# Finding queries without a key by a minimum in the mask instruction of VectorE, with a mask of 0 and 1, scaled queries and reordered instruction lists

## What is computed

```
x = x + attention(layernorm(x), ctx, ctx, mask)      # x 32x56x128, ctx 32x1500x128
x = x + ffn(layernorm(x), w1, w2)                     # 128 -> 512 -> 128, gelu, quantised

q = split(query @ Wq + bq); k = split(ctx @ Wk + bk); v = split(ctx @ Wv + bv)   # 16 heads of 8
scores = q @ k.T / sqrt(8)
scores = where(mask == 0, -1e9, scores)               # mask is int32, 32x1x56x1500
probs  = softmax(scores)
out    = (probs @ v) @ Wo + bo
```

## Time and profile before

| | us |
|---|---|
| median of three executions | 962.15 |
| lowest and highest | 957.84, 962.29 |
| the profiled execution, its own time | 959.75 |
| its span in the profile | 958.0 |

### The profile page before, as it was taken

The page is one execution under the profiler, slowest core; times in us unless marked ns, Lnnn a source line. Parts: engine busy times, 40 slices in busy tenths (PEclk is TensorE's granted clock), DMA queues, the critical chain, the costliest instruction groups (busy, mean ns, idle before and its releaser), DMA issues.

```text
span 958.0 us, 33628 instructions
## 1 busy us (share of the span) xinstructions
PE 887.8 (93%) x11716; PEld 694.2 (72%) x11716; DVE 753.1 (79%) x2593; ACT 673.4 (70%) x1272; POOL 231.5 (24%) x253
## 2 busy tenths in 40 slices
PE   3767989999999999999999999999999999999983
PEld 2344767777787787778787777777787777778772
DVE  3687568888788878888788888888787888888744
ACT  2543667777887877777886777777887777777661
POOL 6310142230222222130222222131222222031200
PEclk9788999999999999999999999999999999999997
DMA  5520221122222211122222211122222111220000
GB/s 130 127 62 1 63 61 29 42 57 60 63 60 63 59 34 47 46 60 60 63 60 63 53 32 50 51 60 60 63 60 61 49 32 50 56 60 0 4 2 6
DMA packets 59375, 49.34 MB, mean 52 GB/s; under 512 B 2785, under 2 KB 55633, under 8 KB 59345
## 3 DMA queue, kind: packets, MB, share of 16 engines
q1 hardware_dynamic: 57551, 48.11, 19.0%
q10 hardware_dynamic: 1793, 0.83, 0.4%
HBM read 47.91 MB, written 0.92 MB: 51 GB/s over the span
## 4 chain that ended last, share of the span: by engine, by line
issue 66%; POOL 18%; PE 7%; DVE 5%; ACT 1%; DMA 1%; POOLq 1%; DVEq 0%; ACTq 0%
POOL k_lo L573 8%; POOL qry_hi L565 4%; POOL qry_lo L566 4%; PE ps_p L820 2%; DMA ctx_sb<-in_ctx_dram 1%; PE ps_p L803 1%; DVE max_junk L1091 1%; POOL q_lo L563 1%; POOL q_hi L562 1%; PE ps_v L856 1%; PE ps_p L744 1%; ACT probs L659 1%; POOL x_rows L581 0%; PE ps_p L741 0%; POOLq L556 0%
## 5 line engine op out<-in xcount | busy, mean ns | idle before, releaser
L1091 DVE CUSTOM_DVE_ANT_0 max_junk<-ps_p,mask_bias 120x500 bf16<-120x500 f32 x768 | 481.6, 675 | 125.3 <-PE ps_p L803 104.5
L659 ACT ACTIVATE probs<-ps_p 125x448 f32<-125x448 f32 x768 | 359.3, 551 | 87.0 <-PE ps_p L820 81.6
L573 POOL TENSOR_TENSOR k_lo<-k_full,k_hi 128x500 fp32r<-128x500 f32 x96 | 119.8, 1262 | 592.0 <-ACT k_hi L651 587.2
L856 PE MATMUL ps_v<-probs,vals 125*32 125x112 f32 x6144 | 162.9, 262 | 0.8 <-issue 0.4
L803 PE MATMUL ps_p<-k_hi,qry_hi 64*120 64x500 f32 x768 | 148.8, 413 | 15.6 <-POOL qry_hi L565 6.5
L820 PE MATMUL ps_p<-qry_hi,k_hi 64*125 64x448 f32 x768 | 158.6, 403 | 4.4 <-DVE seg_max L1091 1.7
L856 PEld LDWEIGHTS ps_v<-probs,vals 125*32 125x32 f32 x6144 | 146.9, 111 | 21.1 <-issue 17.7
L641 ACT ACTIVATE k_full<-ps_p,bk_sb 128x500 f32<-128x500 f32 x96 | 64.7, 674 | 123.1 <-PE ps_p L744 122.6
L820 PE MATMUL ps_p<-own_query,mask_bias 57*125 57x448 f32 x768 | 145.7, 368 | 0.0
L820 PE MATMUL ps_p<-qry_lo,k_hi 64*125 64x448 f32 x768 | 144.4, 366 | 0.0
L820 PE MATMUL ps_p<-qry_hi,k_lo 64*125 64x448 f32 x768 | 144.3, 365 | 0.0
(11 more groups left out here) (124 smaller groups left out, 831.5 us busy)
## 6 DMA issues: line engine op xcount, KB each, us to landing
ctx_sb<-in_ctx_dram SPq DMA_DIRECT2D x31, 750.0 KB
mask_sb<-in_mask_Bx1xSxS_ik_dram SPq DMA_DIRECT2D x64, 328.1 KB
own_query<-shift SPq DMA_DIRECT2D x64, 1.8 KB
out_dram<-x_rows SPq DMA_DIRECT2D x16, 56.0 KB, 1.6
ctx_sb<-in_ctx_dram ACTq DMA_DIRECT2D x1, 750.0 KB
x_rows<-in_x_dram SPq DMA_DIRECT2D x1, 672.0 KB, 10.9
w_sb<-in_L_ffn_w_dram SPq DMA_DIRECT2D x2, 256.0 KB, 8.8
x_rows<-in_x_dram SPq DMA_DIRECT2D x1, 224.0 KB, 5.9
```

The costliest lines, as they stand in the source:

```text
L573: pool.tensor_tensor(k_lo[:, p, at], k_full[:, (p + n) % 2, :], k_hi[:, p, at].bitcast(F32), ALU.subtract)\
L659: act.activation(probs[:, c % NP, h], ps_p[0:KC, BANK[how]["S", c, h], 0:HC], ACT.Exp)\
L856: mm = pe.matmul(ps_v[r:r + VT, col:col + PAIR], vals[:, p, c, t].rearrange("p a r -> p (a r)"), src, start=(c == 0 and t < 4), stop=(c == ...
L1091: dve.tensor_tensor_reduce(max_junk[0:MROWS, BANK[how][slot], :], ps_p[0:MROWS, BANK[how][slot], 0:SEG], mask_bias[0:MROWS, p, s * SEG:(s ...
```

## The change

ScalarE no longer sums the mask. The instruction that turns the mask into a bias also keeps a minimum: it now writes 1 where the mask is 0 and 0 elsewhere, and the minimum over the segment is 1 only if every key is masked. A reduction over the three segments gives `some_key` (which is now 1 for a dead query), and the diagonal `some_diag` is made by one comparison, `ident > some_key`, which is 1 on the diagonal where the query is alive. So `some` now stands behind the third bias of its batch and no longer waits for ACT.

Since the mask is 1 and not -2^30, everything that is added to the scores is brought to that scale: the queries are multiplied by 2^-30 when they are made, the maxima are made with a subtraction, `own_query` has -1 on its diagonal in place of 1 (a second constant, `neg_ident`), `shift` is a plain copy, and ACT's exponential has the scale 2^30.

```
             def bias_mask(bt, n):
...
-                dve.tensor_scalar(mask_bias[0:MROWS + 1, p, at], mask_sb[0:MROWS + 1, p, at], 0.0, -BIG,
-                                  ALU.is_equal, ALU.mult).then_inc(mask_biased, 1)
+                dve.tensor_scalar(mask_bias[0:MROWS + 1, p, at], mask_sb[0:MROWS + 1, p, at], 0.0, None,
+                                  ALU.is_equal, ALU.min, accum_out=all_masked[0:MROWS + 1, n:n + 1])\
+                    .then_inc(mask_biased, 1)
             def find_some(bt):
...
-                dve.wait_ge(mask_summed, b + 1)
-                dve.tensor_scalar(some_key[0:SQ, :], mask_sum[0:SQ, :], 0.5, None, ALU.is_gt)\
-                    .then_inc(some_found, 1)
+                dve.wait_ge(mask_biased, NSEG * (b + 1))
+                dve.tensor_reduce(some_key[0:SQ, :], all_masked[0:SQ, :], AX.X, ALU.min).then_inc(some_found, 1)
                 dve.wait_ge(some_found, b + 1)
-                dve.tensor_scalar(some_diag[0:SQ, :], ident[0:SQ, 0:SQ], some_key[0:SQ, 0:1], None, ALU.mult)\
+                dve.tensor_scalar(some_diag[0:SQ, :], ident[0:SQ, 0:SQ], some_key[0:SQ, 0:1], None, ALU.is_gt)\
                     .then_inc(some_diag_ready, 1)
...
-            def sum_mask(bt):
-
-                b, k, p = bt
-                act.wait_ge(mask_loaded[p], 32 * (k + 1))
-                wait(act, some_found, b)
-                act.activation(mask_sum_junk[0:SQ, :], mask_sb[0:SQ, p, :], ACT.Abs,
-                               accum_out=mask_sum[0:SQ, :]).then_inc(mask_summed, 1)
...
-                act.activation(probs[:, c % NP, h], ps_p[0:KC, BANK[how]["S", c, h], 0:HC], ACT.Exp)\
+                act.activation(probs[:, c % NP, h], ps_p[0:KC, BANK[how]["S", c, h], 0:HC], ACT.Exp, scale=BIG)\
...
-                                      bq_sb[:, 0:1], float(HD) ** -0.5, ALU.add, ALU.mult).then_inc(q_copied, 1)
+                                      bq_sb[:, 0:1], float(HD) ** -0.5 / BIG, ALU.add, ALU.mult).then_inc(q_copied, 1)
...
-                                         ALU.add, ALU.max, seg_max[0:MROWS, 4 * h + r, s:s + 1])\
+                                         ALU.subtract, ALU.max, seg_max[0:MROWS, 4 * h + r, s:s + 1])\
...
+            put(pool.memset(neg_ident[:], 0.0))
+            put(pool.affine_select(out=neg_ident[:], in_=neg_ident[:], compare_op=ALU.not_equal, fill=-1.0,
+                                   base=0, pattern=[[-1, 128]], channel_multiplier=1))
```

```
 DVE_EVEN = order("""
-    own0 m0 m1 m2 m3 m4 m5 m6 m7 m8 m9 bias0 m10 m11 m12 m13 D0 m14 m15 m16 m17 m18 m19 O0 some0 bias1 m20 m21
-    m22 m23 F0 neg0 rows0 R0 rows1 bias2
+    own0 D0 m0 m1 m2 m3 m4 m5 m6 m7 bias0 m8 m9 m10 O0 m11 m12 m13 m14 m15 bias1 m16 m17 m18 m19 bias2 some0 m20
+    m21 m22 m23 neg0 rows0 R0 F0 rows1
...
 POOL_EVEN = order("""
-    kl0 q0 kl1 kl2
+    kl0 kl1 kl2 q0
```

## The result

The changed kernel takes 1011.87 us (median of four runs, 1010.64 to 1013.2), the kernel before 961.01 on the same chip: a ratio of 1.0535, 95% interval 1.0503 to 1.0566. It is 51 us slower. My forecast was 954.5, between 933 and 970.

What follows compares the result with a forecast made beforehand. TensorE, 93% busy, was nearest its limit; VectorE's chain ended the even half, PE's list the odd. 959.75 - 1.5 (loop) - 6.0 (filling) = 952.25 us, put at 954.5 against the median; range 933 to 970.

Steps and rivals of the forecast that it cites:

- the last one of the odd half: From R0 to the next M0 on PE: T1 and 0.25 idle go, D0 (0.3) and 0.45 for own0 enter, 3.1 us.
- rival of mine: Three: row chain slips through, 935 us, 0.34; mask instruction costs 0.9, 970 us, 0.14; no change, 961 us, 0.10.
- The mask instruction: VectorE's mask instruction with accumulated minimum: 0.60 us from start to start, before 0.33; 1.2 us a pass, by cost table 1.6.
- the shared port: VectorE and GpSimd share an exclusively locked port pair; a mask instruction losing its double rate would stop being held.
- The lock: Even half: POOL's last k_lo, qry_hi and qry_lo hold VectorE's row chain, so M0 comes at 27.0 us, before 27.4.
- the 1.0 I left: Even half: VectorE's idle time among its list, 1.0 us where before it was 2.1, putting neg at 18.3 us.
- The pass without the jump: One pass of the loop: 54.1 us, 0.1 less than before, so -1.5 us over 14 passes.
- The even half: From even M0 to odd M0, ended by VectorE's row chain under POOL: 27.0 us, before 27.4.
- The odd half: From odd M0 to even M0: R0 at 24.0 us, then 3.1 to M0, 27.1 us in all.
- the 0.6 that I gave back for a better covered gelu: Odd half: K0, V0 and P0 cover ScalarE's gelu with its table loads, so R0 comes 0.6 us sooner, at 24.0.
- Filling and end: Pipeline filling only: first maxima fill at 26.6 for 30.58 (-4.0 us), three masks moved into lead's list (-2.0), together -6.0.
- faster: The outcome of a time under 957.3 us, given a chance of 0.59.

Runs made afterwards that it cites:

- the padded kernel: The changed kernel with 70 idle instructions more at the start of VectorE's stream, ahead of the loop: 959.56 us, ratio 0.9986 to the kernel before.

## Why the prediction was wrong

**The step that failed** is the last one of the odd half: D0 enters ahead of M0 "with 0.45 for own0, which it must wait for". The new list puts own0 and D0 right behind the branch, and the 0.45 has own0 start there as it did before, after 0.39 us of "issue". It measured 3.06. D0's wait was 2.83 us, not 0.45, and from R0 to M0 it took 6.9 us where I had 3.1 (420.09 to 426.99). In the padded kernel, with the same lists, it is 3.0: the step was right but for the jump. A pass of after takes 58.7 us on average, where I had 54.1. Counted from odd M0 to odd M0, a pass of the padded kernel takes 54.88 us and one of after without a fall of the clock 57.4: 2.5 us for the wait, 33 us over 13 passes. The eight passes with 3.4 us at half clock add 1.4 us each and the three with 6.8 us 2.9, 20 us together. That is 53 of the 53.7 us between the two spans (1011.5 and 957.8). V0's row shows the second part: it takes 1.94 us at 425.12 for 1.05 in the padded kernel. No rival of mine had the jump in it. No row of before has the price of a long jump, and a count of the loop's instructions would have given no more than a warning.

**The mask instruction**: 0.60 from start to start; it is 0.594, and its accumulator read is hidden. Right. Its price of 1.2 to 1.6 us of VectorE's time a pass became 0.22 us of a pass. It has also stopped being held by POOL, as the prediction took it to follow from the shared port: of the 96, four run beside a POOL instruction in after and take 0.67 us like all others, while without the minimum three do, and they take 0.50, 0.87 and 1.46 us where the others take 0.42.

**The lock**: right in kind. L953 and L954 are held by qry_hi and qry_lo, and H waited 1.27 to 1.30 us. VectorE's timeline after:

```profile
453.26 0.87 DVE L953 TENSOR_SCALAR w_sb<-w_sb,row_stat 112x128 f32<-112x128 f32 x1
454.16 1.17 DVE L954 TENSOR_SCALAR w_sb<-w_sb 112x128 bf16<-112x128 f32 x1
```

POOL above it:

```profile
452.91 1.14 POOL L567 TENSOR_TENSOR qry_hi<-head_of_row,q_hi 128x448 fp32r<-128x448 f32 x1 [0.17 <-POOL q_lo L565]
454.12 1.13 POOL L568 TENSOR_TENSOR qry_lo<-head_of_row,q_lo 128x448 fp32r<-128x448 f32 x1
```

Only the first instruction, L944, is not held, which I had expected to be: it comes 23.4 us after M0 in the padded kernel, not 22.3, since VectorE's idle time among the maxima was more than the 1.0 I left.

**The pass without the jump**: 54.83 us, where I said 54.1 and before has 54.15 (over the 13 passes from the second on; the first of the 14 takes 56.6 us before, and my sum took 14 equal ones). The even half came out at 27.26 for 27.0. The odd half came out at 27.60 for 27.1; R0 is 24.6 us after M0, and the 0.6 that I gave back for a better covered gelu was not there.

**Filling and end**: the first maxima fill at 25.8 us, forecast 26.6. By the second pass the padded kernel is 4.3 us ahead (185.5 against 189.8) where I had 6.0. And from the last even M0 to the end it takes 59.5 us in place of 64.2, which I had not considered. The kernel without the minimum shows the same 59.5, so it does not come from the minimum; which move of the new lists does it was not tried. 4.3 + 4.7 - 13 x 0.68 is 0.2 us, the difference of the two spans (957.8 and 958.0).

The result thus rests on one term. Without it my forecast of 954.5 would have stood 5 us off a kernel that is no faster than before, so that "faster" would have been wrong as well: the loop pays back what the filling and the end give.

## What to carry to other kernels

Before a change of order or of instruction count in a loop is priced, count the instructions of its body on each engine, waits and register instructions among them, and look at the profile page's row of instruction packets (13 or 77 here). In this kernel a jump cost next to nothing while the body lay on three blocks, and 2.7 us or more when it touched a fourth. The place of the body counts as well as its length, so instructions ahead of the loop can help or harm. Put nothing that another engine waits for right behind the jump; the 2.1 us of idle time elsewhere in VectorE's list did not pay for it, and a wait of TensorE can cost its clock on top (20 us here). Where another engine holds a small chain, its consumer can be moved back instead of freeing the chain; here the first gave 14 us, the second 12, and both together 20.

## What the runs showed of the hardware

- A loop's jump on VectorE takes 0.22 to 0.28 us while the body touches three blocks of 128 instructions, and 2.7 to 3.0 us when it touches four. Ten more idle instructions at the start of its stream made 959.2 into 1041.9 us. There the body ended about 6 instructions into the fourth block, and the jump took 3.5 to 3.8; why was not tried.
- The jumps of ScalarE (0.21 us, 152 instructions in its body before, 148 now) and of POOL (0.12 us, 34) are as short after as before.
- In the loop of after, one wait of PE of 2.6 to 2.8 us a pass came with 3.4 or 6.8 us at 1.2 GHz in 11 of 13 passes. In the padded kernel waits of 1.3 us at H, one in each pass, came with none. With 40 instructions of padding, waits of 1.5 us at H were followed by 3.4 us at 1.2 GHz in 4 passes.
- A mask instruction that accumulates a minimum takes 0.594 us from start to start for 500 elements, with the read of the accumulator (0.083 us) hidden; one that does not takes 0.33.
